# Third small-head layer: the mask in three bf16 parts, added to all four score banks of a step by 32x32 tiles

## The chip, the cores and the metric

The kernel runs on one core of a Trainium2 chip. It is one launch that computes four attention layers and the MLPs between them. The metric is the device time in microseconds (us). On the core, TensorE (PE in the profile) multiplies matrices, VectorE (DVE), ScalarE (ACT) and GpSimd (POOL) do the element-wise work, and SyncE (SP) issues most of the DMAs; each has its own queue of instructions, and they wait for one another by semaphores. PSUM has eight banks of 128 partitions by 512 float32 values, into which PE accumulates.

## The reference, cut to what matters

Only the last attention layer changes. It has 32 query heads of 8 columns and 8 key heads, for 4 batches of 256 query rows and 256 keys; its additive mask is a full float32 matrix for each batch.

```python
# B = 4, x: (4, 256, 256), encoder states: (4, 256, 256), mask: (4, 1, 256, 256) float32
H, NH, KVH = 256, 32, 8
HD, GROUPS = H // NH, NH // KVH
q = (hidden_state @ Wq + bq).reshape(b, l, KVH, GROUPS, HD).transpose(0, 2, 3, 1, 4)
k = (encoder_hidden_state @ Wk + bk).reshape(b, s, KVH, HD).transpose(0, 2, 1, 3)
v = (encoder_hidden_state @ Wv + bv).reshape(b, s, KVH, HD).transpose(0, 2, 1, 3)
scores = jnp.einsum('bkgld,bksd->bkgls', q, k) * scale
scores = scores + encoder_attention_mask[:, :, None, :, :]
attn = jax.nn.softmax(scores, axis=-1)
out = jnp.einsum('bkgls,bksd->bkgld', attn, v)
out = out.transpose(0, 3, 1, 2, 4).reshape(b, l, H) @ Wo + bo
x = out + hidden_state
return (x - mean(x)) * rsqrt(var(x) + EPS) * gamma + beta
```

## The kernel before

The program runs a first cross-attention with heads of 128, an MLP, and then three layers with small heads (class `Heads`, l = 1, 2, 3), each after an MLP. The third small-head layer is the last 195 us of the program. Its preparation for the first batch (the projections of Q and K, their copies and DMAs) lies in the MLP ahead of it.

**Steps.** The layer works on 4 batches of 32 heads, two heads in a step, so a batch takes 16 steps and the layer has 64 steps, and 5 more for the lag that is described next, followed by two for the end. The scores of a head are computed twice. First `by_query` (L1985) writes them with query rows on the partitions, so that VectorE can take each row's maximum; the bank is one of a ring of three. Five steps later `by_key` (L1999) writes the transposed scores with keys on the partitions into one of two banks, with the row's maximum already in them as extra rows of Q and K; ScalarE takes the exponential of a bank (L2126) and the result is the weight matrix PT for the product with V. So step n holds `by_query` of the two heads of step n and `by_key` of the two heads of step n-5.

**The way of the maxima.** VectorE reduces a head's bank (`maxima`, L2207) into nm; GpSimd turns four heads' values into np (L2239, L2241); PE transposes np (`turn_maxima`, L2061, every even step); ScalarE copies the result to rows (L2140), and GpSimd issues a DMA (L2250) that puts them into the extra rows of Q.

**The mask before.** It is used twice and is in SBUF twice. On the query side M3 is added by VectorE within the maximum: two `tensor_tensor_reduce` for each head (L2207, one for each half of the bank), each followed by a read of the accumulator. On the key side `add_mask` has PE add MT, split into a high and a low fp32r part (MTh, MTl), through an identity matrix of 128x128: two matmuls of 512 columns for each head (L2009, L2010), four in a step. VectorE makes MTh and MTl once per batch (L1660, L1662) one batch ahead: step "maskparts", in the eleventh step of a batch, and for the first batch in the MLP.

**The order of work.** On PE a step from 5 to 63 is `quarters`: for each half, `by_query` of both heads and `by_key` of both heads; then `add_mask`; then, in odd steps, `attend` (L2052: 16 matmuls with tiles of 128x32, two of them for each of eight pairs of a head and a half); then what the tables give for the step. In steps 0 to 4, where there is no `by_key`, a loop `keep_busy` has PE do six matmuls of ones (L2085). On VectorE a step is: the maxima of the first head, the preparation that the table lists for the step before, the finish of the batch before (posts), and the maxima of the second head. The tables IN_MLP and IN_LAYER say at which step of the MLP or of the batch a preparation stands. The posts of a batch lie in steps 6 to 17 of the next one: OS (ScalarE, L2134) is transposed by PE (L1736), divided by VectorE (L1770, On at L1772), transposed again by PE (L178) from the tile On, split, and multiplied with the output weights.

**What waits for what.** `by_query` of head i waits for the maxima of head i-3, `by_key` for the exponential of the head two before it, which used the same bank, the exponential for the last matmul of its bank (semaphore t_st), the maxima for the last matmul of theirs (t_s). SP issues the DMAs in program order: two mask loads for each batch (L1471, L1472) and 24 DMAs (L1465) that lay out Q and K, named Q<-stage and K<-stage in the profile.

## Time and profile before

| what | value |
|---|---|
| median of three runs | 1252.83 us (1250.13 to 1253.26) |
| span of the profiled execution | 1248.4 us |
| PE busy | 1203.5 us, 96% of the span |
| VectorE busy | 888.7 us, 71% |
| ScalarE busy | 779.8 us, 62% |
| GpSimd busy | 598.9 us, 48% |
| steps 0 to 4 of the layer | from 1053.45 us on the trace's clock |
| steps 16 to 31 (second batch) | 44.9 us, of which PE is busy 44.16 |

The span is what the profiler recorded, from the first to the last instruction; it is 4.4 us under the median of the device times, which hold some time around it. All times below that name a moment are microseconds on the clock of this one trace. The rows are read like this: a time is when the instruction began, the next number how long it or its group took, then engine, line of the kernel, operation, output and inputs, and the size of the tile; a bracket gives the idle time ahead of it and what ended it. Matmuls are pipelined: two matmuls of 0.39 us each may begin 0.23 us apart.

### The profile page before, as it was taken

How to read it: one execution, taken by the hardware profiler on the slowest of the kernel's cores; microseconds unless marked ns; L12 is line 12 of the kernel's file. 1: busy time of each engine (PE TensorE's matmuls, PEld its weight loads, DVE VectorE, ACT ScalarE, POOL GpSimd, SP SyncE). 2: the span in 40 equal slices, each digit the busy share in tenths (PEclk: the TensorE clock that was granted, in tenths of full speed). 3: DMA queues.
4: the chain of work that ended last, by engine and by line, in shares of the span. 5: the costliest groups of instructions: out<-in, count | busy, mean ns of one | idle time of the engine just before them, and what ended most of it. 6: DMA issues, size and time to landing. Idle time of an engine off the chain costs nothing.

```text
span 1248.4 us, 27144 instructions
## 1 busy us (share of the span) xinstructions
PE 1203.5 (96%) x9940; PEld 1029.8 (82%) x9940; DVE 888.7 (71%) x2304; ACT 779.8 (62%) x1889; POOL 598.9 (48%) x966
## 2 busy tenths in 40 slices
PE   8999999999999999999989899999999899999997
PEld 7999999999999999999978665786675577666664
DVE  5887877779887777778865787537788464666764
ACT  4876666668876566666874566645676654555553
POOL 3784555548875555454862443504444131324333
PEclk9999999999999999999999999999999999999999
DMA  5540100013431001001420220122222012121100
GB/s 170 153 141 31 35 26 27 27 39 107 142 100 35 27 26 35 27 27 28 126 74 27 81 81 28 51 69 74 84 68 70 10 60 64 54 70 42 40 12 18
DMA packets 56820, 75.03 MB, mean 60 GB/s; under 512 B 11312, under 2 KB 30576, under 8 KB 56688
## 3 DMA queue, kind: packets, MB, share of 16 engines
q1 hardware_dynamic: 51568, 72.75, 19.1%
q8 instruction: 79, 1.29, 0.4%
q0 software_dynamic: 5120, 0.56, 0.3%
...
## 4 chain that ended last, share of the span: by engine, by line
PE 80%; DVE 7%; issue 5%; ACT 4%; POOL 2%; DMA 1%; ACTq 0%; DVEq 0%; POOLq 0%
PE bank L125 19%; PE bank L127 18%; PE bank L126 18%; PE bank L2052 5%; PE bank L771 4%; PE bank L1999 3%; PE bank L2009 3%; PE bank L1985 2%; PE bank L2010 2%; PE bank L1981 1%; ACT PT L2126 1%; DMA Q<-rows 1%; PE bank L178 1%; PE bank L713 1%; PE bank L1736 1%
## 5 line engine op out<-in xcount | busy, mean ns | idle before, releaser
L1095 POOL TENSOR_SCALAR E<-E,rl 128x256 f32<-128x256 f32 x256 | 243.6, 962 | 210.2 <-DVE rl L980 210.2
L2126 ACT ACTIVATE PT<-bank 128x512 f32<-128x512 f32 x320 | 173.5, 594 | 92.6 <-PE bank L2010 56.0
L846 ACT ACTIVATE QTh<-bank,bqs 128x256 fp32r<-128x256 f32 x128 | 60.8, 475 | 156.3 <-PE bank L127 156.2
L2207 DVE CUSTOM_DVE_ANT_0 Em<-bank,M 128x256 bf16<-128x256 f32 x256 | 95.1, 420 | 53.8 <-PE bank L1985 22.3
L856 ACT ACTIVATE E<-bank,nm 128x257 f32<-128x257 f32 x256 | 119.5, 481 | 1.2 <-DVE nm L950 1.0
L984 DVE TENSOR_TENSOR PTl<-bank,PTh 128x512 fp32r<-128x512 f32 x128 | 88.0, 688 | 27.3 <-ACT PTh L868 26.8
L957 DVE SCALAR_TENSOR_TENSOR QTl<-bank,bqs,QTh 128x256 fp32r<-128x256 f32 x128 | 61.6, 481 | 64.0 <-ACT KT L847 63.2
L868 ACT CAST PTh<-bank 128x512 fp32r<-128x512 f32 x128 | 75.2, 588 | 43.2 <-PE bank L771 43.2
L2201 DVE TENSOR_REDUCE nm<-bank 128x1 f32<-128x512 f32 x128 | 83.3, 685 | 23.5 <-PE bank L1981 22.3
L950 DVE TENSOR_REDUCE nm<-bank 128x1 f32<-128x257 f32 x256 | 95.5, 414 | 3.6 <-PE bank L127 3.6
L1999 PE MATMUL bank<-Q,K 51*128 51x256 f32 (+1 forms) x640 | 85.2, 315 | 4.9 <-DMA Q<-rows 2.4
L2052 PE MATMUL bank<-PT,V 128*32 128x256 f32 x1280 | 86.6, 400 | 1.8 <-ACT PT L2126 1.8
L125 PE MATMUL bank<-KT,QTh 128*128 128x258 f32 x256 | 83.4, 326 | 3.3 <-issue 3.0
L2255 POOL DMA_DIRECT2D Q<-rows x96 | 54.5, 569 | 65.5 <-ACT rows L2140 65.1
L771 PE MATMUL bank<-ident,E 128*128 128x128 f32 x512 | 76.7, 272 | 0.0
L1999 PEld LDWEIGHTS bank<-Q,K 51*128 51x128 f32 (+1 forms) x640 | 60.0, 187 | 19.4 <-ACT PT L2126 8.5
L990 DVE SCALAR_TENSOR_TENSOR OTl<-bank,cols,OTh 128x256 fp32r<-128x256 f32 x128 | 60.8, 475 | 18.1 <-ACT OTh L874 18.1
L126 PE MATMUL bank<-KT,QTh 128*128 128x258 f32 x256 | 73.2, 286 | 0.0
L2250 POOL DMA_DIRECT2D Q<-rows x64 | 36.9, 579 | 74.0 <-ACT rows L2140 71.2
L127 PE MATMUL bank<-KT,QTl 128*128 128x258 f32 x256 | 72.1, 282 | 0.0
L125 PE MATMUL bank<-PTh,Vh 128*128 128x256 f32 x256 | 71.8, 280 | 0.0
L127 PE MATMUL bank<-PTh,Vl 128*128 128x256 f32 x256 | 71.6, 280 | 0.0
...
## 6 DMA issues: line engine op xcount, KB each, us to landing
...
K<-stage SPq DMA_DIRECT2D x48, 128.0 KB
Q<-stage SPq DMA_DIRECT2D x48, 128.0 KB
...
K<-xh SPq DMA_DIRECT2D x16, 128.0 KB, 3.0
Q<-rows POOLq DMA_DIRECT2D x96, 4.0 KB, 1.7
```

The source lines that it names most:

```text
L125: pe.matmul(o, wh, xh, start=first, stop=False, skip_group_check=skip)
L126: pe.matmul(o, wh, xl, start=False, stop=False, skip_group_check=skip)
L127: return pe.matmul(o, wl, xh, start=False, stop=last, skip_group_check=skip)
L771: m = pe.transpose(s.PTB[:, k * 256 + t * 128:k * 256 + t * 128 + 128], s.E[:, i % 3, t, k * 128:k * 128 + 128], c.ident[:])
L856: m = act.activation(s.E[:, i % 3, t, 0:257], bank[:, 0:257], ACT.Exp, bias=s.nm[:, r, t:t + 1], accum_out=s.ls[:, r, t:t + 1])
L950: dve.tensor_reduce(s.nm[:, r, t:t + 1], bank[:, 0:257], AX.X, ALU.max, negate=True).then_inc(S["dve_max"])
L984: dve.tensor_tensor(s.PTl[:], s.PTB[:].rearrange("p (a b) -> p a b", a=2), f32(s.PTh[:]), ALU.subtract).then_inc(S["dve_pt"])
L1095: m = pool.tensor_scalar(s.E[:, i % 3, t, 0:256], s.E[:, i % 3, t, 0:256], s.rl[:, r, t:t + 1], None, ALU.mult)
L1999: z = pe.matmul(s.STB[y][:, 256 * e:256 * e + 256], s.K[r][at, q // s.rp, o:o + 128], s.Q[r][at, q // s.blocks, :], start=l != 3 or e == 0 ...
L2052: z = pe.matmul(s.OB[32 * q:32 * q + 32, 0:256], s.V[b % s.NV][:, k, (4 * g + q) // s.rep, :], s.PT[(i0 + q) % s.NPT][:, k, :], start=k == ...
L2126: act.activation(s.PT[i % s.NPT][:, 2 * u:2 * u + 2, :].rearrange("p a b -> p (a b)"), s.STB[y][:], ACT.Exp).then_inc(S["t_ex"])
L2207: dve.tensor_tensor_reduce(out=s.Em[:, (2 * i + e) % 4], in0=bank[:, e * 256:e * 256 + 256], in1=s.M3[:, j, e, :], scale=-1.0, scalar=3.4e ...
```

## The change

The mask is now added by PE on both sides, in three bf16 parts that together hold the float32 value.

- VectorE makes the parts: `parts0` for the query side and `parts1` for the key side, four instructions of 128x512 each (a maximum with a large negative number into bf16, a subtraction, a copy to bf16, a subtraction), into the tile MP. The mask is loaded into M2, one copy for all batches.
- SP lays the parts out by 16 DMAs a batch (`mask_out`) from MP into MS, so that each group of 32 partitions holds the whole mask of one side: groups 0 and 1 the query side, groups 2 and 3 the key side. One DMA has 32 partitions by three parts by 512 bf16 values, 96 KB. There are two MS, which the batches use in turn.
- `add_masks` replaces `add_mask`: for each part, for each block k of 32 output partitions and for each bank (two of `by_query`, two of `by_key`) one matmul with a tile of 32x32 and 512 columns, 48 in a step and 24 in steps with heads on one side alone. The banks' semaphores are raised by each bank's last matmul, which are the last four of the 48.
- The maximum is one `tensor_reduce` of the whole bank for each head, and its semaphore goes up once for each head.
- The tables move the steps: in the MLP the load from place 3 to 2, and the parts and `mask_out` stand at place 8; in a batch the load moves from step 0 to 7, `parts0` stands at step 10, `parts1` at 11, `mask_out` at 12.

```diff
-            3: {0: ["mask", "turn", "th", "tl", "res"], 2: ["q0"], 3: ["q1", "qh", "ql"], 5: ["k0", "kh", "kl"],
-                6: ["q_out", "k_out"], 8: ["v0", "v1", "va"], 10: ["maskparts"]}}
+            3: {0: ["turn", "th", "tl", "res"], 2: ["q0"], 3: ["q1", "qh", "ql"], 5: ["k0", "kh", "kl"],
+                6: ["q_out", "k_out"], 7: ["mask"], 8: ["v0", "v1", "va"], 10: ["parts0"], 11: ["parts1"], 12: ["mask_out"]}}
...
+    elif x == "mask_out" and l == 3:
+        w.wait_ge(S["mask_low"], 2 * b + 2)
+        if b >= 2:
+            w.wait_ge(S["t_s"], s.o["s"] + (b - 1) * s.nh)
+            w.wait_ge(S["t_st"], s.o["st"] + (b - 1) * s.nh)
+        for k in range(4):
+            for a in range(4):
+                sp.dma_start(s.MS[j][32 * a:32 * a + 32, :, k, :], s.MP[32 * k:32 * k + 32, :, a // 2, :]
+                             ).then_inc(S[f"dma_ms{j}"], 16)
...
-        dve.tensor_scalar(s.MTh[:, j, :], raw, BIG, None, ALU.max).then_inc(S["mask_high"])
-        w.wait_ge(S["mask_high"], b + 1)
-        dve.scalar_tensor_tensor(out=s.MTl[:, j, :], in0=raw, scalar=BIG, in1=f32(s.MTh[:, j, :]), op0=ALU.max,
-                                 op1=ALU.subtract).then_inc(S["mask_low"])
+    if x in ("parts0", "parts1"):
+        kind = int(x[-1])
+        raw, part, n = s.M2[:, kind, :], s.MP[:, :, kind, :], 2 * b + kind + 1
+        w.wait_ge(S[f"ld_m3{kind}"], 16 * (b + 1))
+        if b:
+            w.wait_ge(S[f"dma_ms{1 - j}"], 256 * ((b - 1) // 2 + 1))
+        dve.tensor_scalar(part[:, 0], raw, BIG, None, ALU.max).then_inc(S["mask_high"])
+        w.wait_ge(S["mask_high"], n)
+        dve.scalar_tensor_tensor(out=raw, in0=raw, scalar=BIG, in1=part[:, 0], op0=ALU.max, op1=ALU.subtract
+                                 ).then_inc(S["mask_rest"])
+        w.wait_ge(S["mask_rest"], n)
+        dve.tensor_copy(part[:, 1], raw).then_inc(S["mask_mid"])
+        w.wait_ge(S["mask_mid"], n)
+        dve.tensor_tensor(part[:, 2], raw, part[:, 1], ALU.subtract).then_inc(S["mask_low"])
...
-        w.wait_ge(S["mask_low"], b + 1)
-        w.wait_ge(S["ident_r"], 1)
-        pe.matmul(bank[:], s.identR[:], s.MTh[:, b % 2, :], start=False, stop=False, skip_group_check=True)
-        pe.matmul(bank[:], s.identR[:], s.MTl[:, b % 2, :], start=False, stop=True, skip_group_check=True
-                  ).then_inc(S["t_st"])
+        groups = [(y, n // s.TB, s.SB[k % len(s.SB)], "t_s") for y, k in enumerate(s.in_step(n))]
+        groups += [(2 + y, (n - s.L) // s.TB, s.STB[y], "t_st") for y, k in enumerate(s.in_step(n - s.L))]
+        w.wait_ge(S["ident_b"], 4)
+        for part in range(3):
+            for k in range(4):
+                for a, b, bank, done in groups:
+                    at, to = slice(32 * a, 32 * a + 32), slice(32 * k, 32 * k + 32)
+                    w.wait_ge(S[f"dma_ms{b % 2}"], 256 * (b // 2 + 1))
+                    z = pe.matmul(bank[to, :], s.units32[at, :], s.MS[b % 2][at, part, k, :], start=False,
+                                  stop=part == 2, skip_group_check=True)
+                    if part == 2 and k == 3:
+                        z.then_inc(S[done])
...
+        if l != 2:
             dve.tensor_reduce(nm, bank[:].rearrange("p (a b) -> p a b", a=2), AX.X, ALU.max, negate=True
                               ).then_inc(S["t_mx"])
...
-            for e in range(2):
-                w.wait_ge(S["t_mx"], s.o["mx"] + 2 * i + e - 3)
-                dve.tensor_tensor_reduce(out=s.Em[:, (2 * i + e) % 4], in0=bank[:, e * 256:e * 256 + 256],
-                                         in1=s.M3[:, j, e, :], scale=-1.0, scalar=3.4e38, op0=ALU.add,
-                                         op1=ALU.min, accum_out=nm[:, e:e + 1]).then_inc(S["t_mx"])
```

Ahead of it in the MLP, and again between two batches, SP's queue shows where the layout stands. This is SP's queue before, from the loads of the first batch's mask to the layout of the second batch's Q and K (MT is the transposed mask):

```order
L1471 DMA M_135_17876<-in_mask 128x2x256
L1472 DMA MT_17877<-in_mask3t 128x2x256
L1481 DMA vb_17880<-in_rows 128x256
L1482 DMA ob_17881<-in_rows 128x256
L1465 DMA K_17874<-stage_54 8x8x256 x12
L1465 DMA Q_17873<-stage_54 8x8x256 x12
L1936 DMA gam_18611<-in_rows 128x256
L1937 DMA bet_18612<-in_rows 128x256
L1471 DMA M_135_17876<-in_mask 128x2x256
L1472 DMA MT_17877<-in_mask3t 128x2x256
L1465 DMA Q_18592<-stage_54 8x8x256 x12
L1465 DMA K_18593<-stage_54 8x8x256 x12
```

And this is the same stretch now, with one batch's end more (MS is the laid-out mask, MP its parts, M_136 the tile M2):

```order
L1465 DMA K_17874<-stage_54 8x8x256 x12
L1489 DMA MS_17876<-MP_17878 32x3x512 x16
L1465 DMA Q_17873<-stage_54 8x8x256 x12
L1950 DMA gam_18639<-in_rows 128x256
L1951 DMA bet_18640<-in_rows 128x256
L1465 DMA Q_18620<-stage_54 8x8x256 x12
L1465 DMA K_18621<-stage_54 8x8x256 x12
L1470 DMA M_136_17877<-in_mask 128x2x256
L1470 DMA M_136_17877<-in_mask3t 128x2x256
L1489 DMA MS_18637<-MP_17878 32x3x512 x16
```

Sixteen DMAs stand between the layouts of K and of Q in the MLP, and in each batch the mask's loads moved behind the layout of K, with 16 more DMAs behind them.

On VectorE, this is where the mask of the third batch was made before, between the maxima of the first and of the second head of a step (nm are the maxima, bank a score bank, OTl a post of the batch before):

```order
L2207 ISA Em_18604,nm_18601<-bank,M_135_17876 128x256
L2207 ISA nm_18601 128x1
L1660 TENSOR_SCALAR MTh_17878<-MT_17877 128x512
L1662 SCALAR_TENSOR_TENSOR MTl_17879<-MT_17877,MTh_17878 128x512
L1777 TENSOR_TENSOR OTl_18610<-bank,OTh_18609 128x512
L2207 ISA Em_18604,nm_18601<-bank,M_135_17876 128x256
L2207 ISA nm_18601 128x1
```

Now two groups of four stand there, in this step and in the next:

```order
L2219 TENSOR_REDUCE nm_18629<-bank 128x2 x2
L1670 TENSOR_SCALAR MP_17878<-M_136_17877 128x512
L1672 SCALAR_TENSOR_TENSOR M_136_17877<-M_136_17877,MP_17878 128x512
L1675 CAST MP_17878<-M_136_17877 128x512
L1677 TENSOR_TENSOR MP_17878<-M_136_17877,MP_17878 128x512
L1791 TENSOR_TENSOR OTl_18636<-bank,OTh_18635 128x512
L2219 TENSOR_REDUCE nm_18629<-bank 128x2 x2
L1670 TENSOR_SCALAR MP_17878<-M_136_17877 128x512
L1672 SCALAR_TENSOR_TENSOR M_136_17877<-M_136_17877,MP_17878 128x512
L1675 CAST MP_17878<-M_136_17877 128x512
L1677 TENSOR_TENSOR MP_17878<-M_136_17877,MP_17878 128x512
L2219 TENSOR_REDUCE nm_18629<-bank 128x2 x2
```

Both groups have the maxima of one head ahead of them and those of the other behind, and the post (L1791) waits for the first group.

On PE, this is the end of the scores of one odd step before, with its masks and the first `attend` matmuls:

```order
L1999 MATMUL bank3<-Q_142_18592,K_143_18593 128x256
L1999 MATMUL bank4<-Q_142_18592,K_143_18593 128x256
L2009 MATMUL bank3<-MTh_137_17878,identR_155_18605 128x512
L2010 MATMUL bank3<-MTl_138_17879,identR_155_18605 128x512
L2009 MATMUL bank4<-MTh_137_17878,identR_155_18605 128x512
L2010 MATMUL bank4<-MTl_138_17879,identR_155_18605 128x512
L2052 MATMUL bank0<-PT_145_18595,V_144_18594 32x256
```

Now the same place reads as follows, and the last four rows come twelve times in all:

```order
L2013 MATMUL bank3<-Q_141_18620,K_142_18621 128x256
L2013 MATMUL bank4<-Q_141_18620,K_142_18621 128x256
L2029 MATMUL bank6<-MS_158_18637,units32_159_18638 32x512
L2029 MATMUL bank1<-MS_158_18637,units32_159_18638 32x512
L2029 MATMUL bank3<-MS_158_18637,units32_159_18638 32x512
L2029 MATMUL bank4<-MS_158_18637,units32_159_18638 32x512
```

Banks 6 and 1 are those of `by_query` (L1985 before), which now get the mask too, ahead of the banks of `by_key` in each group of four.

## Rows read from the trace of the kernel before

**Rows 1.** Windows of the last layer: us, busy of each engine, PEclk, DMA, GB/s

```profile
1092.00:1136.90 44.90, 44.16 (x398) 28.51 (x394) 30.62 (x151) 24.27 (x53) 14.32 (x35) 1.00 0.18 50
...
1234.30:1248.40 14.10, 7.12 (x60) 5.16 (x60) 5.69 (x16) 2.58 (x6) 2.27 (x4) 0.87 0.06 19
```

**Rows 2.** Last layer by line and shape: busy, mean ns, idle before

```profile
L2207 DVE CUSTOM_DVE_ANT_0 Em<-bank,M 128x256 bf16<-128x256 f32 x256 | 95.1, 420 | 53.8 <-PE bank L1985 22.3 <-POOL np L2241 19.7 <-issue 11.6
L2126 ACT ACTIVATE PT<-bank 128x512 f32<-128x512 f32 x128 | 69.5, 595 | 56.0 <-PE bank L2010 56.0
...
L2052 PE MATMUL bank<-PT,V 128*32 128x256 f32 x512 | 34.3, 385 | 0.7 <-ACT PT L2126 0.7
```

**Rows 3.** Timeline of PE, steps 10 and 11

```profile
1077.30 0.39 PE L1985 MATMUL bank<-K,Q 24*128 24x256 f32 x2
...
1077.74 0.50 PE L2009 MATMUL bank<-MTh,identR 128*128 128x512 f32 x1
...
1078.98 0.38 PE L1985 MATMUL bank<-K,Q 24*128 24x256 f32 x2
1079.25 0.78 PE L1999 MATMUL bank<-Q,K 26*128 26x256 f32 x2
...
1080.08 0.51 PE L2009 MATMUL bank<-MTh,identR 128*128 128x512 f32 x1
1080.42 0.39 PE L2010 MATMUL bank<-MTl,identR 128*128 128x512 f32 x1
1080.65 0.40 PE L2009 MATMUL bank<-MTh,identR 128*128 128x512 f32 x1
...
1081.20 1.07 PE L2052 MATMUL bank<-PT,V 128*32 128x256 f32 x16
1082.21 0.39 PE L1985 MATMUL bank<-K,Q 24*128 24x256 f32 x2
```

**Rows 4.** Timeline of ScalarE and of VectorE, steps 10 and 11

```profile
1078.51 1.09 ACT L2126 ACTIVATE PT<-bank 128x512 f32<-128x512 f32 x2 [0.70 <-PE bank L2010]
...
1080.77 0.42 DVE L1660 TENSOR_SCALAR MTh<-MT 128x512 fp32r<-128x512 f32 x1
1081.22 0.69 DVE L1662 SCALAR_TENSOR_TENSOR MTl<-MT,MTh 128x512 fp32r<-128x512 f32 x1
```

**Rows 5.** Timeline of VectorE in the first small-head layer

```profile
723.09 1.88 DVE L2198 TENSOR_REDUCE nm<-bank 128x2 f32<-128x512 f32 x3
```

**Rows 6.** Timeline of PE around steps 0 and 1 of the last layer

```profile
1053.45 0.50 PE L1985 MATMUL bank<-K,Q 24*128 24x256 f32 x4
...
1056.20 1.47 PE L2085 MATMUL bank<-units 128*128 128x512 bf16 x6
```

**Rows 7.** Queue of SP, its issues from 1030 to 1100

```profile
1039.67 7.76 SPq L1465 DMA_DIRECT2D Q<-stage  x12
...
1091.36 0.37 SPq L1471 DMA_DIRECT2D M<-in_mask  x1
```

**Rows 8.** DMA issues of the page: KB each, us to landing

```profile
K<-xh SPq DMA_DIRECT2D x16, 128.0 KB, 3.0
Q<-rows POOLq DMA_DIRECT2D x96, 4.0 KB, 1.7
```

**Rows 9.** Timeline of a post of step 58, VectorE and PE

```profile
1209.65 0.29 DVE L1772 TENSOR_TENSOR On<-bank,rl 128x128 f32<-128x128 f32 x1
...
1209.99 0.66 PE L178 MATMUL bank<-ident,On 128*128 128x128 f32 x4 [0.33 <-DVE On L1772]
```

**Rows 10.** Timeline of the MLP ahead of the layer, VectorE and PE

```profile
1032.01 0.68 DVE L475 TENSOR_TENSOR GL<-G,GH 128x512 fp32r<-128x512 f32 x1
...
1034.13 0.37 PE L125 MATMUL bank<-W7x,GH 128*128 128x256 f32 x1
```

**Rows 11.** Timeline and window of PE at the other clock, an earlier layer

```profile
783.31 0.47 PE L125 MATMUL bank<-hTh,W3x 128*128 128x512 f32 x1 [1.77 <-DVE hTl L418]
...
784.00:787.40 3.40, 3.40 (x21) 1.30 (x19) 0.00 (x0) 0.74 (x2) 0.00 (x0) 0.50 0.02 5
```

More of the change, by code:

```diff
@@ L1163 @@
               12: ["x_out", "v2", "v3", "vb"]},
-          3: {3: ["mask"], 6: ["k0", "kh", "kl"], 7: ["v0", "v1", "va", "k_out"], 8: ["maskparts"],
+          3: {2: ["mask"], 6: ["k0", "kh", "kl"], 7: ["v0", "v1", "va", "k_out"], 8: ["parts0", "parts1", "mask_out"],
               9: ["turn", "th", "tl", "res"], 10: ["q0", "q1", "qh", "ql"], 11: ["q_out"]}}
@@ L1247, in take_first @@
         if self.l == 3:
-            self.M3, self.MT = sb("M3", [128, 2, 2, 256]), sb("MT", [128, 2, 2, 256])
-            self.MTh, self.MTl = sb("MTh", [128, 2, 512], F32R), sb("MTl", [128, 2, 512], F32R)
+            self.MS = [sb("MS", [128, 3, 4, 512], BF16)]
+            self.M2 = sb("M2", [128, 2, 512])
+            self.MP = sb("MP", [128, 3, 2, 512], BF16)
         else:
@@ L1277, in take_rest @@
         if self.l == 3:
+            self.MS.append(sb("MS", [128, 3, 4, 512], BF16))
+            self.units32 = sb("units32", [128, 32], BF16)
             self.gam, self.bet = sb("gam", [128, 256]), sb("bet", [128, 256])
@@ L1371, in mx @@
     def mx(self, i):
-        return self.o["mx"] + i * (1 if self.l == 1 else 2)
+        return self.o["mx"] + i * self.units
 def spread_done(c, w, l):
@@ L1467, in heads_prep_sp @@
     if x == "mask" and l == 3:
-        if b >= 2:
-            w.wait_ge(S["t_mx"], s.mx((b - 1) * s.nh))
-            w.wait_ge(S["mask_low"], b - 1)
-        sp.dma_start(s.M3[:, j], dram["mask3"][b].rearrange("(t p) s -> p t s", p=128)).then_inc(S[f"ld_m3{j}"], 16)
-        sp.dma_start(s.MT[:, j], dram["mask3t"][b].rearrange("(s p) t -> p s t", p=128)).then_inc(S[f"ld_mt{j}"], 16)
+        w.wait_ge(S["mask_low"], 2 * b)
+        for kind, src in enumerate((dram["mask3"], dram["mask3t"])):
+            sp.dma_start(s.M2[:, kind, :].rearrange("p (e c) -> p e c", e=2),
+                         src[b].rearrange("(e p) c -> p e c", p=128)).then_inc(S[f"ld_m3{kind}"], 16)
     elif x == "mask":
@@ L1978, in by_query @@
         bank = s.SB[n % len(s.SB)]
-        w.wait_ge(S["t_mx"], s.o["mx"] + (n - len(s.SB) + 1) * (2 if l == 3 else 1))
+        w.wait_ge(S["t_mx"], s.o["mx"] + n - len(s.SB) + 1)
         if l == 2:
@@ L1985, in by_query @@
             z = pe.matmul(bank[:, 256 * e:256 * e + 256], s.Q[r][at, q // s.blocks, 128 * e:128 * e + 128],
-                          s.K[r][at, q // s.rp, :], start=True, stop=True)
-        if 1 in es:
+                          s.K[r][at, q // s.rp, :], start=l != 3 or e == 0, stop=l != 3, skip_group_check=l == 3)
+        if l != 3 and 1 in es:
             z.then_inc(S["t_s"])
@@ L2002, in by_key, with add_masks @@
             z.then_inc(S["t_st"])
-    def add_mask(n):
-        b, bank = n // (s.WD * s.TB), s.STB[n % 2]
-        w.wait_ge(S["mask_low"], b + 1)
-        w.wait_ge(S["ident_r"], 1)
-        pe.matmul(bank[:], s.identR[:], s.MTh[:, b % 2, :], start=False, stop=False, skip_group_check=True)
-        pe.matmul(bank[:], s.identR[:], s.MTl[:, b % 2, :], start=False, stop=True, skip_group_check=True
-                  ).then_inc(S["t_st"])
+    def add_masks(n):
+        groups = [(y, n // s.TB, s.SB[k % len(s.SB)], "t_s") for y, k in enumerate(s.in_step(n))]
[10 more added lines that the diff above has]
+                        z.then_inc(S[done])
     def fours(n):
@@ L2036, in quarters @@
                 by_key(k, e)
-        for k in s.in_step(n - s.L):
-            add_mask(k)
+        add_masks(n)
     def attend(gi, k, n):
@@ L2144, in heads_act @@
         w.wait_ge(S["ld_ident"], 16)
-        act.copy(s.identR[:], c.ident[:]).then_inc(S["ident_r"])
+        for k in range(0, 128, 32):
+            act.copy(s.units32[k:k + 32, :], c.ident[k:k + 32, k:k + 32]).then_inc(S["ident_b"])
     for n in range(s.steps()):
```

17 lines of the change are left out of this document (2 added, 15 removed).

## The prediction, made before the run

> **What bounds the kernel now.** I read the windows of the last layer first. In the sixteen steps of the second batch PE is busy 44.16 of 44.90 us at the full granted clock, level 2.4 GHz [rows 1]; the other three engines are busy 14 to 31 us. So what PE is given costs time at once, and what VectorE is spared gives nothing unless PE waits for it. The groups by line then tell whom PE waits for: the exponentials wait 56.0 us for the second mask matmul, PE before the products only 0.7 us for the exponentials [rows 2]. The timeline of two steps shows the rhythm: an even step starts at 1077.30, the odd one at 1078.98, the next even one at 1082.21, 4.91 us for the pair [rows 3]. In it one loop closes: masks from 1077.74, exponentials 1078.51 to 1079.60, and only then the second `by_key` of the odd step, which is why its group of two takes 0.78 us [rows 3, 4].
>
> **The mask phase of a step.** Before it is four matmuls of 512 columns through the whole array, spaced 0.34 us after a change of tile shape and 0.23 us otherwise: 1080.08, 1080.42, 1080.65, to 1081.20 where the products start, 1.12 us; in the even step 1077.74 to 1078.78, 1.04 [rows 3]. The change makes 48 matmuls of 512 columns, each in a sixteenth of the array. bf16 matmuls of 512 columns follow each other 0.22 us apart: six take 1.47 with the last one's 0.4 [rows 6]. If sixteen tiles run side by side, 48 are three rounds, 0.65 us; I add 0.13 for the starts and weight loads and 0.09 for the change of tile shape (from 0.34 against 0.23), 0.87 us. That no row shows more than four tiles at once makes this the weakest number. Bound below: 0.65. Bound above: only four at once, 12 rounds of 0.22, 2.6 us. I take 0.87, nearest to the rows that show four tiles of `by_query` and `by_key` side by side at the rate of one (two groups of two start at 1077.30 and the masks 0.44 us later).
>
> So a step's PE work falls by 0.17 to 0.25 us, yet the exponentials come later. Both key banks are now finished by the last of the 48, about 0.98 us after the masks' start, where the first bank was ready after 0.77 (1078.51). The loop above grows by 0.21 and shrinks by the shorter phase of 0.25: 0.04 us for a pair, nothing. The gain of the phase is eaten, because the order is by part and not by bank.
>
> **Steps 0 to 4.** `by_query` alone gets 24 matmuls a step where there was no mask: I take 0.87 for each of five steps, **+4.3** (bounds 3.3, five times three bare rounds of 0.22, and 6.6, six rounds each if four run at once).
>
> **The maxima.** A head costs 0.84 plus two accumulator reads before, that is two starts each 0.35 apart, 1.38 us for the step [rows 2]; a `tensor_reduce` of 128x2 from 128x512 takes 0.60 us from one to the next (three in 1.88, the last of them 0.68) [rows 5], 1.20. VectorE saves 0.18 us a step but begins 0.9 later, at the end of the mask phase, step start + 1.5 against + 0.63. Where a post then needs VectorE, PE meets it. In step 58, On ends at 1209.94 and PE's transpose starts at 1209.99, after 0.33 us idle [rows 9]. In the second to fourth batch this comes in four steps: the two even ones grow by 0.75, the two odd ones, which have products ahead, by 0.4: 2.3 for each of three batches.
>
> **The parts.** On VectorE a 128x512 maximum takes 0.45 with its gap and a subtraction 0.72 [rows 4]. Four instructions, 0.45 + 0.72 + 0.45 + 0.61, are 2.2 us for a kind and 4.5 for both, against 1.06.
> - In the MLP the GL of 1032.01 comes behind them. It ends at 1032.69, PE takes it up at 1034.13 [rows 10], a slack of 1.4; 3.3 later means **+1.9** (bounds 0 and 3.4).
> - In steps 11 and 12 of the first batch 3.4 us more stand before the second heads' maxima, and the turned maxima of the next even step wait for these: **+1.8** (bounds 0 and 3.4). The same in the second and third batch, 2.1 each, since their posts (OTl) wait too. With the 2.3 above that is 4.4 for each, **+8.8**; the last batch has no next, 2.3, and about 1.1 for five last steps whose key masks are 0.21 later with nothing beside them, **+3.4**.
>
> **The layout by DMA.** SP issues 12 DMAs of Q<-stage in 7.76 us, 0.65 each [rows 7]; a mask load takes 0.37 [rows 7], 0.42 with a gap. The landing is 3.0 us for 128 KB between tiles, 1.7 for 4 KB [rows 8]. MS has 96 KB in 96 rows, so I take 0.65 and 3.0; the bounds are 0.42 and 1.7.
> - In the MLP 16 of them stand ahead of Q's 12. The parts end at 1035.5, 16 take until 1045.9, Q's 12 until 1053.7 where they began at 1039.67 before, and land at 1056.7. The layer would start at 1053.45 + 1.9 = 1055.35 [rows 6, 7]: **+1.3** (0 with the quick issue).
> - At steps 16, 32 and 48 PE needs the next batch's MS. From the start of step 11 (1078.98): its masks wait 1.1 us behind the scores (1080.08), t_s comes at 2.45, the first head's reduce ends at 3.05, `parts0` at 5.25, the second head's reduce and step 12's first one at 6.45, `parts1` at 8.7. SP then issues, the last one after 15 x 0.65 at 18.4, and it lands at 21.4. PE arrives at the masks of step 16 after 13.0 us (1078.98 to 1092.00 [rows 1, 3]), + 1.9 for the growth of these steps, + 0.44 for its scores: 15.3. It idles 6.1, I take 6.0 three times, **+18**. Low bound: 15 x 0.42 and 1.7 give 16.7, 1.4 us. High: 7. Behind the waiting matmul stands all of PE's queue, the products of older heads too, and so the whole layer.
> - PE's clock: after an idle of 1.77 us at 783.31 [rows 11], the window from 784.0 to 787.4 has the granted clock 0.50, the 1.2 GHz level, for 3.4 us of work that takes half. Three idles of 6 us could each be followed by that: 1.5 each, **+4.5** (bounds 0 and 9). The layer's end, where PE is busy 7.12 of 14.10 us, has 0.87 already [rows 1].
>
> The sum, against the profiled execution: 1.9 + 1.3 + 4.3 + 1.8 + 18 + 8.8 + 3.4 + 4.5 = 44.0 on a span of 1248.4, 1292.4. The median lies 4.4 over the span: 1296.8, **1297 us**.
>
> **The rivals.**
> - *The layout is there in time, or nearly* (C, 0.12): a quick issue, three waits of 1.4 instead of 6 and no clock loss: 1297 - 14 - 4.5 - 1.3 = 1277. For it: the loads at 1091.36 are issued in 0.37 [rows 7]. Against: DMAs with many short pieces took 0.65.
> - *Sixteen tiles cost more than they stream* (D, 0.10): each of 48 matmuls occupies PE by itself. The products are 16 matmuls in 1.07 us, 0.05 from one to the next with the last one's 0.3 taken off [rows 3]; at half of that 48 take 1.2 and with the change of shape 1.35, 0.5 over my phase. 64 steps: +32, 1329. The Trainium skill, TensorEngine Tiling (Array Packing), section Instruction Overhead, gives about 60 cycles a matmul, which would be an estimate of 1.2 us for 48; the page TensorE: Matmul & The Clock Gate, part on packing, has sixteen tiles of 512 columns at 10.6 times one, which speaks for the short phase. No row here has sixteen tiles, so by the second page the sum stays, by the first it is 1329.
> - *Only four tiles run at once* (E, 0.08), as the rows show four and no more: 12 rounds of 0.22, 2.6 us, 1.7 over my phase, in 64 steps 110, and it pulls five first steps and the VectorE chain behind it: about 1297 + 110 = 1407.
> - *Faster* (F, 0.08): if the layout lands before step 16, and PE's 0.2 us a step (64 x 0.2 = 13) does count because the exponentials keep up, the rest being 4.3 + 1.9: 1253 - 13 + 6 = 1246, or less if the first steps hide in what were `keep_busy` matmuls, 1243. It decides at the landing: the sixteenth DMA must land within 15.3 us of step 11's start. Against it is the chain of 21.4.
> - *No difference* (0.04): the same with the posts' waits, within 1249 and 1257.
>
> **How the numbers follow.** My case has 0.58 and by itself 1280 to 1314. Range: C's 1277 less 1.9 (MLP), 1.8 (first parts), 1.0 (first steps), half of the 8.8, and 4 if 0.06 us of the phase's gain stays in each step, is 1264. D's 1329 plus the high bounds, 3 (layout), 4.5 (clock), 1.6 (first parts), 1.5 (MLP), 2.3 (first steps) and 3 if the queue of Q is as much slower, is 1345. Outside stand E, F and no difference, 0.20. A measurement of this kernel tells about 0.3% (3.8 us) from no change: faster 0.08, same 0.04, slower 0.88.
>
> **What would show it.** Right: PE idle of some 6 us ahead of the first L2029 in steps 16, 32 and 48, ended by MS<-MP; sixteen issues of 0.65 us; sets of 48 that take 0.8 to 0.9 us to the next matmul; exponentials about 1 us after the masks' start; `tensor_reduce` 0.60 apart, four part instructions of 2.2 us; GL waits in the MLP; a clock under 1.00 after the idles. Wrong: a mask phase over 1.2 us (D, E); a landing under 15 us after step 11 (C, F); a pair of steps that falls from 4.91 to under 4.6 us.

## The result and the profile after

The changed kernel takes 1305.28 us, the median of four runs (1304.86 to 1305.91), against 1253.05 for the kernel before, measured beside it. The ratio is 1.043 (95% interval 1.041 to 1.045): slower by 52 us, where 44 were forecast (1297, range 1264 to 1345). The profiled execution has a span of 1303.4 us, 55.0 more than before.

The page of the changed kernel, its busy line, three of its groups (line, engine, output and inputs, count, busy us and mean ns, idle time ahead and who ended it) and the issue of the layout:

```profile
PE 1221.3 (94%) x12756; PEld 1030.8 (79%) x12756; DVE 890.8 (68%) x1944; ACT 777.1 (60%) x1892; POOL 599.7 (46%) x966
...
L2146 ACT ACTIVATE PT<-bank 128x512 f32<-128x512 f32 x320 | 173.5, 594 | 145.2 <-PE bank L2029 108.4
L2219 DVE TENSOR_REDUCE nm<-bank 128x2 f32<-128x512 f32 x192 | 126.9, 684 | 118.0 <-PE bank L2029 101.9
...
L2029 PE MATMUL bank<-MS,units 32*32 32x512 bf16 x3072 | 69.4, 418 | 19.0 <-DMA MS<-MP 18.3
...
MS<-MP SPq DMA_DIRECT2D x64, 96.0 KB, 2.2
```

PE is busier by 18 us than before and yet 2 points less of the span. The exponentials of the three layers wait 145.2 us, 92.6 before, and 108.4 of it is for the mask matmuls of L2029; the maxima of the first and third layer wait 118.0, 101.9 of it for the same, which now finish every bank of the third layer; and the layout MS lands 2.2 us after its issue.

The layer is best read by the starts of its steps (the first `by_query` matmul of a step in each trace). In us, for the profiled executions, with "e1" and the like for the experiments told below:

| steps | before | after | difference | forecast | e1 early | e3 no query | e8 filled | e6a order |
|---|---|---|---|---|---|---|---|---|
| start of the layer | 1053.5 | 1057.1 | +3.7 | +3.2 | 1057.0 | 1060.1 | 1058.3 | 1055.6 |
| 0 to 4 | 10.3 | 14.7 | +4.4 | +4.3 | 14.7 | 10.9 | 10.9 | 14.0 |
| 5 to 15 | 28.2 | 31.0 | +2.7 | +1.8 | 34.5 | 40.8 | 33.5 | 29.2 |
| 16, 32 and 48 | 6.2 | 27.6 | +21.5 | +18 | 7.8 | 9.3 | 8.2 | 6.4 |
| 17 to 31 | 42.8 | 49.0 | +6.2 | +4.4 | 46.9 | 58.7 | 47.6 | 42.5 |
| 33 to 47 | 43.0 | 50.3 | +7.4 | +4.4 | 46.4 | 50.9 | 42.6 | 43.3 |
| 49 to the end | 64.4 | 73.6 | +9.1 | +3.4 | 69.4 | 79.7 | 69.4 | 70.0 |

The forecast's last term, 4.5 us for the clock, has no row of its own; it sits in the rows from 16 on.

Windows of the changed kernel: steps 5 to 15, the three steps at which a new batch begins, the layer's end from step 63, and a part of it (us; busy us of PE, weight loads, VectorE, ScalarE, GpSimd; granted clock, DMA share, GB/s):

```profile
1071.90:1102.80 30.90, 27.90 (x720) 15.95 (x719) 20.57 (x37) 14.29 (x33) 8.91 (x22) 0.94 0.35 91
1102.80:1113.30 10.50, 3.52 (x65) 1.88 (x61) 1.09 (x3) 1.57 (x4) 0.38 (x2) 0.74 0.44 90
1162.30:1170.50 8.20, 3.30 (x66) 1.75 (x62) 1.31 (x3) 1.41 (x3) 1.51 (x4) 0.71 0.46 98
1220.80:1229.90 9.10, 2.65 (x62) 1.19 (x58) 1.22 (x4) 0.70 (x3) 2.32 (x5) 0.67 0.50 103
1270.40:1303.40 33.00, 24.40 (x306) 13.33 (x305) 10.80 (x30) 9.85 (x22) 8.72 (x16) 0.78 0.06 18
1281.30:1294.00 12.70, 10.90 (x100) 5.16 (x101) 1.07 (x4) 3.33 (x7) 0.00 (x0) 0.53 0.02 7
```

In the second to fourth window, the steps at which a new batch begins, PE works 3.5, 3.3 and 2.7 us out of 10.5, 8.2 and 9.1, where it was busy 44.16 of 44.90 in the sixteen steps of [rows 1]. And the clock, which was at 1.00 there before, has fallen: 0.74, 0.71 and 0.67 in these, and 0.53 in the 12.7 us from 1281.30, in which PE is busy 10.90 us. The timeline of PE around step 16, step 15's masks and products ahead of it (start, us, line, tile, the bracket with the idle time and who ended it):

```profile
1098.41 0.92 PE L2029 MATMUL bank<-MS,units 32*32 32x512 bf16 x48
1099.26 0.28 PE L2081 MATMUL bank<-ident,np 128*16 128x128 f32 x1
...
1101.00 0.92 PE L2029 MATMUL bank<-MS,units 32*32 32x512 bf16 x48
1101.85 1.07 PE L2072 MATMUL bank<-PT,V 128*32 128x256 f32 x16
...
1110.63 1.51 PE L2029 MATMUL bank<-MS,units 32*32 32x512 bf16 x48 [6.98 <-DMA MS<-MP]
```

The 48 tile matmuls take 0.92 us to the last one's end and 0.85 to the next instruction (1098.41 to 1099.26, 1101.00 to 1101.85), where four whole-array ones took 1.04 and 1.12 [rows 3]. One after another, 0.22 us apart [rows 6], 48 would take 10.6 us, so the sixteen tiles do run side by side. Then PE waits 6.98 us for MS. The last 1.51 us row is the same work at the other clock. SP's queue, in the MLP and from the first batch on:

```profile
1035.37 11.82 SPq L1489 DMA_DIRECT2D MS<-MP  x16
1047.24 7.86 SPq L1465 DMA_DIRECT2D Q<-stage  x12
...
1096.28 12.70 SPq L1489 DMA_DIRECT2D MS<-MP  x16
```

Sixteen DMAs of 96 KB take 11.82 and 12.70 us to issue, 0.74 and 0.79 each; K and Q take 0.65 [rows 7].

### The profile page after: what moved, and what is told of

It is laid out like the page before. It is cut to its first block, busy times and chain, and to the rows that moved or that the text cites. A ratio compares the mean times of both kernels' runs of the same rounds, so it can differ in the third digit from the quotient of the medians.

```text
span 1303.4 us, 32384 instructions
## 1 busy us (share of the span) xinstructions
PE 1221.3 (94%) x12756; PEld 1030.8 (79%) x12756; DVE 890.8 (68%) x1944; ACT 777.1 (60%) x1892; POOL 599.7 (46%) x966
## 4 chain that ended last, share of the span: by engine, by line
PE 76%; DVE 8%; issue 5%; ACT 4%; SPq 4%; DMA 2%; POOL 1%; DVEq 0%; ACTq 0%; POOLq 0%
PE bank L125 18%; PE bank L127 17%; PE bank L126 17%; PE bank L2072 5%; PE bank L771 4%; PE bank L2029 3%; PE bank L2013 3%; SPq L1489 2%; PE bank L1999 2%; DMA Q<-rows 2%; PE bank L178 1%; PE bank L1995 1%; DVE nm L2219 1%; PE bank L1750 1%; PE bank L713 1%
## 5 line engine op out<-in xcount | busy, mean ns | idle before, releaser
L2146 ACT ACTIVATE PT<-bank 128x512 f32<-128x512 f32 x320 | 173.5, 594 | 145.2 <-PE bank L2029 108.4
L2219 DVE TENSOR_REDUCE nm<-bank 128x2 f32<-128x512 f32 x192 | 126.9, 684 | 118.0 <-PE bank L2029 101.9
L2013 PE MATMUL bank<-Q,K 51*128 51x256 f32 (+1 forms) x640 | 92.0, 325 | 5.8 <-DMA Q<-rows 3.2
L2072 PE MATMUL bank<-PT,V 128*32 128x256 f32 x1280 | 90.8, 415 | 2.3 <-ACT PT L2146 2.3
L2029 PE MATMUL bank<-MS,units 32*32 32x512 bf16 x3072 | 69.4, 418 | 19.0 <-DMA MS<-MP 18.3
L2013 PEld LDWEIGHTS bank<-Q,K 51*128 51x128 f32 (+1 forms) x640 | 64.6, 193 | 21.7 <-ACT PT L2146 7.0
```

Of the source, the lines that this page charges most:

```text
L2013: z = pe.matmul(s.STB[y][:, 256 * e:256 * e + 256], s.K[r][at, q // s.rp, o:o + 128], s.Q[r][at, q // s.blocks, :], start=l != 3 or e == 0 ...
L2029: z = pe.matmul(bank[to, :], s.units32[at, :], s.MS[b % 2][at, part, k, :], start=False, stop=part == 2, skip_group_check=True)
L2072: z = pe.matmul(s.OB[32 * q:32 * q + 32, 0:256], s.V[b % s.NV][:, k, (4 * g + q) // s.rep, :], s.PT[(i0 + q) % s.NPT][:, k, :], start=k == ...
L2146: act.activation(s.PT[i % s.NPT][:, 2 * u:2 * u + 2, :].rearrange("p a b -> p (a b)"), s.STB[y][:], ACT.Exp).then_inc(S["t_ex"])
L2219: dve.tensor_reduce(nm, bank[:].rearrange("p (a b) -> p a b", a=2), AX.X, ALU.max, negate=True).then_inc(S["t_mx"])
```

## Experiments

**e1, the layout earlier.** In the tables of the third layer:

```diff
-            3: {0: ["turn", "th", "tl", "res"], 2: ["q0"], 3: ["q1", "qh", "ql"], 5: ["k0", "kh", "kl"],
-                6: ["q_out", "k_out"], 7: ["mask"], 8: ["v0", "v1", "va"], 10: ["parts0"], 11: ["parts1"], 12: ["mask_out"]}}
+            3: {0: ["mask", "turn", "th", "tl", "res"], 2: ["q0"], 3: ["q1", "qh", "ql", "parts0"], 4: ["parts1"],
+                5: ["k0", "kh", "kl"], 6: ["q_out", "k_out"], 7: ["mask_out"], 8: ["v0", "v1", "va"]}}
```

> The changed kernel with the layout earlier and nothing else: the mask's load at step 0 of a batch, parts0 at step 3, parts1 at 4, the 16 DMAs at step 7, right behind the layout of K. Theory A (PE waits for the layout at steps 16, 32 and 48, by 7.1, 4.7 and 6.5 us in the changed kernel's trace, 18.3 in all, and the clock that falls to 1.2 GHz around these idles costs some us more): 1305 falls by 18 to 26, to 1279 to 1287, with no wait for MS at the three steps. Rival B (the transfers only collide with something else, the layout of Q and K or the maxima's rows, wherever they stand): a fall of under 8 us, and waits for Q<-rows or K at the same steps.

Measured: 1278.93 us (1278.08 to 1281.24), 26 under the changed kernel; ratio to the kernel before 1.023 (1.020 to 1.025). Steps 16, 32 and 48 fall from 27.6 to 7.8 us, and no wait for MS is left at them. SP begins the layout at 1085.72 instead of 1096.28:

```profile
1085.72 12.20 SPq L1489 DMA_DIRECT2D MS<-MP  x16
```

So theory A holds, at the edge of its range of 1279 to 1287. The price is where it said nothing: the parts stand in steps 3 and 4 of the tables, which VectorE works off in steps 4 and 5, and steps 5 to 10 take 19.3 us instead of 15.5; the granted clock is 0.50 from 1077.0 to 1083.8, so a part of this is the clock's. The maxima's rows come later at two places too. PE in steps 14 and 15:

```profile
1100.40 0.92 PE L2029 MATMUL bank<-MS,units 32*32 32x512 bf16 x48
...
1103.12 0.39 PE L2013 MATMUL bank<-Q,K 26*128 26x256 f32 x2 [0.56 <-DMA Q<-rows]
```

GpSimd issued these rows at 1097.76, when SP had just issued the last of the 16 DMAs (1097.92) and began with the loads of the next mask (1097.96 and 1098.60). Such rows land after 2.0 us in the median of this run and 3.6 at most; whether the layout or the loads hold them up is not shown. With a second wait, of 1.18 us at 1170.78, this is 1.7 us in all; the changed kernel has one such wait, of 1.03 us at 1183.49, and the kernel before none. It is rival B's mechanism at a small size: A is the main thing and B a small one.

**e3, no mask on the query side.** `groups` holds the key side alone, and `by_query` ends its bank itself:

```diff
-        groups = [(y, n // s.TB, s.SB[k % len(s.SB)], "t_s") for y, k in enumerate(s.in_step(n))]
-        groups += [(2 + y, (n - s.L) // s.TB, s.STB[y], "t_st") for y, k in enumerate(s.in_step(n - s.L))]
+        groups = [(2 + y, (n - s.L) // s.TB, s.STB[y], "t_st") for y, k in enumerate(s.in_step(n - s.L))]
```

> The changed kernel, but the mask is left out of the query side on PE, so that the maxima are those of the unmasked scores; the key side keeps its 24 tile matmuls a step, and all parts and DMAs stay. Theory A (24 of 48 matmuls cost only where the key side has none, in steps 0 to 4, 4.4 us; and the maxima start about 1 us earlier in each step, which frees the posts and the parts, 6 to 9 us, and lets the layout start up to 1.5 us earlier at each of three boundaries): 1287 to 1294, with the mask phase of a step 0.77 against 0.85. Rival B (48 tile matmuls cost twice what 24 do): the phase falls to about 0.45 and the time to under 1280.

Measured: 1310.66 us (1308.90 to 1320.10). Half of the tile matmuls are gone and the kernel is not faster but 5 us slower; neither theory had that. Steps 0 to 4 did fall to 10.9 us, by 3.8 where 4.4 were expected. But steps 5 to 15 rose from 31.0 to 40.8. The mask phase of 24 matmuls at the beginning and a few steps later:

```profile
1072.11 0.84 PE L2028 MATMUL bank<-MS,units 32*32 32x512 bf16 x24
...
1081.21 1.48 PE L2028 MATMUL bank<-MS,units 32*32 32x512 bf16 x24
```

It is 0.84 us with the last one's own time in the first row, and 0.77 to the next instruction (1072.88), as theory A had it. In the second it is 1.48: the same 24 matmuls at half the clock. A window ahead of the fall of the clock, the one behind it, and two windows of 80 us, from 18 us after the layer's start:

```profile
1071.80:1076.80 5.00, 4.67 (x77) 2.57 (x78) 4.07 (x8) 2.64 (x6) 1.33 (x4) 1.00 0.37 101
1076.80:1128.00 51.20, 51.20 (x557) 22.29 (x556) 21.82 (x37) 18.33 (x40) 12.19 (x30) 0.50 0.26 64
...
1078.10:1158.10 80.00, 79.09 (x876) 36.48 (x868) 33.27 (x64) 29.73 (x65) 15.95 (x42) 0.54 0.26 66
1158.10:1238.10 80.00, 77.35 (x1044) 37.57 (x1028) 48.31 (x94) 33.80 (x75) 26.77 (x62) 0.71 0.32 75
```

The clock falls after 5 us in which PE was busy 4.67, and stays at 0.50 for 51.2 us in which PE is never idle. Over the first 80 us PE is busy 79.09 at a granted clock of 0.54. So it is not idle time that keeps the clock low here.

**e8, the same with whole-array matmuls added.**

```diff
-        if l < 3:
-            fill_step(n)
+        fill_step(n)
...
-        ones(s.OB, 1 if posts else 2)
+        ones(s.OB, (1 if posts else 2) if l < 3 else 3)
```

> The run without masks on the query side (1310.7 us, clock 0.93) with three whole-array matmuls of ones added in every step from 5 that has no products, preparation or last post on PE: about 0.65 us of added work in some 25 steps, 16 us in all. Theory A (24 small tiles in a step leave too much of the array idle, and the granted clock falls to 0.50 for that): the clock of the layer rises to 0.9 or more and the time falls by 20 to 45 us, to 1266 to 1290, although PE is given more work. Rival B (the clock fell for another reason, such as idle time of PE): the clock stays where it was and the time rises to 1315 to 1330.

Measured: 1261.16 us (1256.71 to 1271.96), 49.5 us less than without the filling. The trace has 57 more matmuls of ones, 19 steps of three. At 0.22 us each that is 12.5 us of work that nobody needs. The same two windows, again from 18 us after the layer's start:

```profile
1076.30:1156.30 80.00, 76.43 (x1127) 37.06 (x1119) 47.53 (x91) 37.09 (x83) 22.48 (x57) 0.83 0.33 80
1156.30:1236.30 80.00, 77.03 (x1313) 39.36 (x1310) 50.97 (x98) 41.45 (x95) 28.87 (x69) 1.00 0.26 63
```

The clock is 0.83 and 1.00 where it was 0.54 and 0.71. The filling did not hold it everywhere: from 1092.1 to 1119.4 (steps 13 to 19) it is 0.50, with PE busy all the time. The profiled run is the slowest of the four. Theory A holds, and the fall in time is larger than the 20 to 45 us that it said.

**e5, the control.** The kernel before with a plain maximum:

```diff
-                dve.tensor_tensor_reduce(out=s.Em[:, (2 * i + e) % 4], in0=bank[:, e * 256:e * 256 + 256],
-                                         in1=s.M3[:, j, e, :], scale=-1.0, scalar=3.4e38, op0=ALU.add,
-                                         op1=ALU.min, accum_out=nm[:, e:e + 1]).then_inc(S["t_mx"])
+            dve.tensor_reduce(nm, bank[:].rearrange("p (a b) -> p a b", a=2), AX.X, ALU.max, negate=True
+                              ).then_inc(S["t_mx"])
```

> The kernel before, with one change: the maximum is one plain reduction of a head's bank (the mask is left out on the query side); the key side keeps its masks through the whole 128x128 array. It differs from the run without masks on the query side (1310.7 us, clock 0.93) in that the key side's masks are whole-array matmuls and not tiles of 32x32, and nothing is laid out. Theory A (VectorE hardly bounds the layer, and the low clock of that other run comes from the tile matmuls in place of whole-array ones): 1247 to 1253 and a clock of 1.00 through the layer. Rival B (the clock fell there because the maxima, or their being early, changed the rhythm): a clock under 1.00 in the layer here too, and over 1265.

Measured: 1248.89 us (1247.34 to 1250.85, ten runs), ratio 0.9991 (0.9979 to 1.0003): no difference.

```profile
1071.70:1151.70 80.00, 79.06 (x701) 50.28 (x701) 48.83 (x91) 44.14 (x98) 28.89 (x68) 1.00 0.18 51
1151.70:1231.70 80.00, 78.58 (x686) 48.98 (x679) 45.25 (x93) 41.66 (x91) 28.67 (x68) 1.00 0.10 27
```

The clock is 1.00, with PE as busy as in e3 (79.06 against 79.09 of 80 us). Two things follow. The cheaper maximum, which the change has too, is worth nothing that can be told: VectorE was not in the way. And what sets e3 apart from this is the form of the key side's masks: four fp32r matmuls through the whole array here, 24 bf16 ones through eight of sixteen tiles there. The parts and their DMAs are a second difference, but e8 has them too and is at 1.00 in its second window.

**e4, one part of three.** `for part in range(1)`, so 16 matmuls a step.

> The changed kernel with one of the three parts added, the other two left out (16 matmuls a step instead of 48); parts and DMAs all stay. Theory A (the three parts are three rounds of 0.22 us and the exponentials wait for the last one, so each step is 0.42 shorter): the mask phase is 0.42 instead of 0.85, a pair of steps falls from 4.88 to about 4.0, but PE comes earlier to the same layout at three boundaries and waits about 2 us more there: 1280 to 1287. Rival B (the phase is hidden behind the exponentials, which bound the loop): a pair stays over 4.6 and the time over 1297.

Measured: 1288.61 us (1281.10 to 1294.01), a little over theory A's range. The phase is what it said, 0.36 to the next instruction:

```profile
1096.01 0.43 PE L2029 MATMUL bank<-MS,units 32*32 32x512 bf16 x16
1096.37 1.07 PE L2072 MATMUL bank<-PT,V 128*32 128x256 f32 x16
```

The pair of steps 14 and 15 falls from 4.88 to 4.25, not to 4.0. Rival B falls: the phase is on the path. The gain is not whole, since steps 16, 32 and 48 still take 25.4 us, and the clock of the whole execution is 0.954 against 0.970. Fewer tile matmuls again come with a lower clock; what causes it was not tested here.

**e7, the end of the layer filled.**

```diff
+        if l == 3 and s.T < n < s.T + s.L:
+            w.wait_ge(S["t_mx"], s.o["mx"] + s.T * s.WD)
+            ones(s.SB[0], 3)
```

> The changed kernel with three matmuls of ones added ahead of the scores of steps 65 to 68, where PE waits for the exponentials; in the changed kernel the granted clock is 0.50 from about 1282 to 1295. Theory A (the clock falls because PE idles 0.8 us there and the tile matmuls of 24 a step don't keep it up): the clock stays at 1.00, and the stretch from step 63 to the end falls from 33.0 us to 28 to 30, so 1301 to 1303 in all. Rival B (the clock falls for what happened before, or whatever the filling): unchanged within 1 us, or slower by the 2.6 us that the filling takes.

Measured: 1304.05 us (1301.36 to 1305.87), ratio to the kernel before 1.042 against 1.043; that alone can't be told from no change. From step 63 to the end it is 30.7 us (from 1269.3) instead of 33.0. The window from step 63 on:

```profile
1269.30:1299.90 30.60, 22.85 (x318) 12.77 (x317) 10.77 (x30) 9.74 (x22) 8.72 (x16) 0.93 0.06 19
```

Its clock is 0.93, where that of the changed kernel, from 1270.40, is 0.78. So the clock is higher there with the filling, if not the 1.00 of theory A, and 2.3 us come back out of the 5.2 that this end had lost, not 3 to 5.

**e6a, posts ahead of maxima, parts in halves.** With e1's early layout; on VectorE:

```diff
+        if l < 3:
             for k in s.in_step(n)[:s.WD - 1]:
                 maxima(k)
...
         for x in steps:
             heads_post_dve(c, s, b, x)
+        if l == 3:
+            for k in s.in_step(n)[:s.WD - 1]:
+                maxima(k)
```

> The changed kernel with the early layout (1278.9 us by itself), and on VectorE the preparations and posts of a step ahead of the first head's maxima and the parts split in halves over four steps (two instructions in each). Theory A (in the changed kernel PE waits in the post steps, since On comes behind maxima that start about 1 us later; and the early parts cost 3.9 us in steps 5 to 10): the waits for On go, steps 54 to 58 fall from 16.1 to 14.0 to 14.5 us, steps 5 to 10 from 19.3 to under 16: 1262 to 1270 in all. Rival B (the maxima are what PE waits for, so that moving them behind the posts costs as much): 1276 to 1284.

Measured: 1264.65 us (1262.49 to 1267.78). In the changed kernel On comes behind the first head's maximum, and PE's transpose (L1750) waits for it, here in step 24:

```profile
1136.30 0.29 DVE L1786 TENSOR_TENSOR On<-bank,rl 128x128 f32<-128x128 f32 x1
...
1136.65 0.66 PE L1750 MATMUL bank<-ident,OS 128*128 128x128 f32 x4 [1.34 <-DVE On L1786]
```

In e6a the same transpose of step 24 waits 0.29 us, and that of step 56 stands right behind the masks, with no wait:

```profile
1122.97 0.66 PE L1752 MATMUL bank<-ident,OS 128*128 128x128 f32 x4 [0.29 <-DVE On L1788]
...
1210.81 0.92 PE L2031 MATMUL bank<-MS,units 32*32 32x512 bf16 x48
1211.66 0.66 PE L1752 MATMUL bank<-ident,OS 128*128 128x128 f32 x4
```

Steps 54 to 58 fall from 16.1 to 13.2 us, under the 14.0 of the kernel before, and steps 5 to 10 are back at 15.4. Theory A holds in both places.

**e6b, the parts earlier in the MLP and fewer ones.** e6a with the parts at places 4 and 5 of the MLP, and `ones(s.STB[1], 3)` instead of 6.

> As the run before with two more changes: in the MLP ahead the parts are made earlier, so that the 16 DMAs of the first mask start right behind those of K (1032 and not 1035), and in steps 0 to 4 three matmuls of ones instead of six. Theory A: the layer starts 2 to 3 us earlier, and steps 0 to 4 take 11.5 to 12.5 us instead of 14.7, since the masks of the query side now keep PE busy: 5 us under the run before, 1257 to 1265, still not under the kernel before. Rival B (with fewer whole-array matmuls the clock falls to 0.50 in the steps behind): 3 us or more over theory A's time, with a clock under 1.00 between steps 2 and 10.

Measured: 1265.76 us (1264.00 to 1266.09), no gain. Steps 0 to 4 take 12.1 us, as expected, but the layer starts at 1060.2, 4.7 us later than in e6a and not 2 to 3 earlier. PE in the MLP:

```profile
1022.00 0.38 PE L125 MATMUL bank<-W7x,GH 128*128 128x256 f32 x1 [2.98 <-DVE GL L475]
...
1026.84 0.50 PE L125 MATMUL bank<-mhTh,W6x 128*128 128x512 f32 x1 [3.15 <-DVE mhTl L418]
```

The parts stand ahead of another GL and of mhTl there; the two waits are 2.98 and 3.15, where e6a has 1.61 for mhTl and 2.76 for its GL. These are 1.8 of the 4.7 us. Another 2.0 are not from the edit: from 993.3 to 1000.1, before the parts, this execution has a granted clock of 0.50 where that of e6a has 1.00, and a matmul that starts at 1013.17 in e6a starts at 1015.49 here, 2.3 us later, of which 0.4 were there before. In the layer some windows of 5 us between steps 4 and 13 have a clock of 0.66 to 0.85, as rival B had said, but its 3 us over theory A's time (1257 to 1265) are not there. The medians of e6a and e6b are 1.1 us apart, and the runs of e6a alone spread over 5.3, so the two can't be told apart.

**e9, what was left of both.** e6a with three ones at the start and e7's filling at the end.

> The run with the early layout, the posts ahead of the maxima and the parts in halves (1264.7 us), with three matmuls of ones instead of six in steps 0 to 4 and three more ahead of the scores of steps 65 to 68. Theory A (the two gains are independent: steps 0 to 4 take 12.1 us instead of 14.0, as in the run that also moved the parts in the MLP, and the end of the layer takes 29 to 31 us instead of 32.8 with the clock kept up): 1258 to 1262. Rival B (each matmul of ones taken out at the start comes back as a lower clock behind it): 1263 to 1268 with a clock under 1.00 in steps 5 to 15. Either way it stays above the kernel before (1250 to 1253), since the first steps, the parts in the MLP and the pairs of plain steps (5.17 us against 4.90) each still cost more.

Measured: 1261.71 us (1261.07 to 1270.62), ratio 1.012 (1.008 to 1.016). Steps 0 to 4 take 12.9 us, not 12.1, and the end 30.3. Theory A's time (1258 to 1262) holds; the clock is 1.00 in steps 5 to 15, so rival B falls. It lies 44 us under the changed kernel and 12 over the kernel before; none of the versions with tile matmuls beats that one.

## Why the prediction was right, step by step

- **The mask phase**, the number called weakest, was right: 0.85 measured for 0.87 (0.92 with the last matmul's end). Rivals D and E fall with it. Here the trace bears out the second page of the Trainium skill that the prediction weighed, TensorE: Matmul & The Clock Gate (part on packing), and not the 60 cycles for each matmul of the Trainium skill's TensorEngine Tiling (Array Packing), section Instruction Overhead: 48 starts take 0.54 us, 11 ns each.
- **Its effect on the pairs was mis-sized, and the sign was wrong.** The prediction let the loop grow by 0.21 and shrink by 0.25 and took nothing. The exponentials indeed start about 1.0 us after the masks:

```profile
1099.43 1.09 ACT L2146 ACTIVATE PT<-bank 128x512 f32<-128x512 f32 x2 [0.94 <-PE bank L2029]
...
1102.02 1.09 ACT L2146 ACTIVATE PT<-bank 128x512 f32<-128x512 f32 x2 [1.38 <-PE bank L2029]
```

  From the masks' start at 1101.00 to the exponentials' end at 1103.11 it is 2.11 us, 1.86 before, so 0.25 more. With 0.47 us from there to the next masks the loop takes 2.58. Before, only the odd step of a pair was held by it (2.34 from masks to masks) and the even one by PE's own work (2.56), 4.90 in all. Now both steps are, and twice 2.58 is the 5.17 us of the plain pairs in e1 and e6a (steps 10 to 13, say). A faster PE can't shorten a loop in which the result comes later. The plain pairs so lose up to 0.27 each, and the steps with posts, where PE is the bound, gain: in e6a steps 22 to 26 take 13.9 against 15.2.
- **Steps 0 to 4**: +4.4 for +4.3.
- **The parts in a batch**: the pair of steps 12 and 13 takes 7.2 us for 4.9 before, 2.3 more for the 1.8 forecast; the granted clock is 0.50 in part of it.
- **The MLP**: +3.7 for +3.2, by the mechanism told. The 3.7 hide a lead: ahead of the parts the changed kernel's trace runs 0.6 us early (the same matmul starts at 1014.39, before at 1014.98), so the MLP itself costs 4.3. VectorE's four instructions for a kind and GL behind eight of them:

```profile
1030.36 0.41 DVE L1670 TENSOR_SCALAR MP<-M 128x512 bf16<-128x512 f32 x1
1030.81 0.69 DVE L1672 SCALAR_TENSOR_TENSOR M<-M,MP 128x512 f32<-128x512 f32 x1
1031.54 0.43 DVE L1675 CAST MP<-M 128x512 bf16<-128x512 f32 x1
1032.00 0.69 DVE L1677 TENSOR_TENSOR MP<-M,MP 128x512 bf16<-128x512 f32 x1
...
1035.27 1.21 DVE L475 TENSOR_TENSOR GL<-G,GH 128x512 fp32r<-128x512 f32 x1
```

  GL ends at 1036.48, 3.8 us later than before [rows 10], and PE waits 2.76 (forecast 1.9). The eight instructions take 4.9 us for the 4.5 forecast, and GL itself 1.21 where it took 0.68. The queue of Q begins at 1047.24 (forecast 1045.9).

```profile
1036.53 0.58 PE L125 MATMUL bank<-W7x,GH 128*128 128x256 f32 x1 [2.76 <-DVE GL L475]
```

- **The three boundaries**: waits of 6.98, and by the starts of the masks (5.45 and 7.26 us into steps 32 and 48, against 0.73 without a wait) 4.7 and 6.5, 18.2 in all for 18. That the sum is so near is in part luck, for errors cancel: the issue takes 0.74 to 0.79 and not 0.65, the landing 2.2 and not 3.0, and PE comes to step 16's masks 1.0 us later than forecast. e1 showed the cause by taking it away.
- **The posts**: the wait for On is 1.34 us in step 24, 1.0 more than the 0.32 of the kernel before there, for the 0.75 forecast. e1, with the early layout alone, keeps the 1.34; e6a, which also has the other order and the halved parts, has 0.29.
- **The clock** was the term that was too small. 4.5 us stood for three stretches behind the idles. In the trace low stretches also lie elsewhere (0.74 in 1095 to 1100, 0.66 in 1195 to 1205, 0.53 in 1281.3 to 1294.0), and the end of the layer alone grew by 5.2 us, a place where the prediction had only 1.1 and steps of posts. A window ahead of one such fall, and the one behind it:

```profile
1191.60:1196.60 5.00, 3.39 (x77) 2.63 (x74) 2.59 (x6) 1.57 (x4) 0.38 (x2) 1.00 0.30 79
1196.60:1203.40 6.80, 6.80 (x96) 3.63 (x96) 2.01 (x6) 1.71 (x4) 1.52 (x4) 0.50 0.41 125
```

  In the steps of the layer and at its end the clock is at 0.50 for 55.6 us, and PE is busy 44.0 of them, 15.0 at the three boundaries and 29.0 elsewhere; before, PE had no work in the layer at that level. If all of it took half the time at 1.00, the clock would cost 22 us. That is an estimate from above, since a set of 48 masks grew only from 0.92 to 1.51. In the changed kernel PE was busy 0.75 to 4.40 of the 5 us ahead of each fall, so idle time and tiles are not told apart in it. e3, e8 and e5 show that it isn't idle time alone: the clock stayed at 0.50 with PE busy all the time when half of the tile matmuls were gone, and it rose when whole-array matmuls were added. Most of what the sum lacks lies where the clock is low: 5.7 us in the last row of the table, 3.5 at the three boundaries and 3.0 in steps 33 to 47, against the 4.5 set down for the clock.
- **No difference, C and F** fall: the layout was there 23.3 us after step 11's start at 1087.35 (forecast 21.4) and PE after 16.3 (forecast 15.3), so the layout came 7 us after PE, and 8 us after F's point of decision at 15.3. e1 makes F's condition true and is still slower by 28 us, so F was wrong in a second step too: the rest of the change is not a gain with the layout in time.

The result is nearer to the forecast than the sum is. The spans differ by 55.0 us where the sum had 44.0, so it was short by 11; the medians differ by 52.2, so the forecast was short by 8. The difference is in the 4.4 us put between span and median: in the changed kernel and in every experiment the profiled run's time is 1.3 to 1.6 over its span, so the span of 1248.4 belongs in all likelihood to the fastest of the three runs before (1250.13), 2.7 under their median. Measured beside the experiments, the kernel before has medians of 1249.8 to 1251.0 and not 1253.05, against which the change costs some 55 us.

How much of the 52 us is the clock can't be told exactly, since clock and waits change one another. What the runs give: e1 takes away 26 with the layout, e6a another 14 with VectorE's order and the halves; some 12 us remain, of which the profiled run of e6a has 2 at the layer's start, 4 in steps 0 to 4 and 5 at its end.
